# First attention: the order of four projections on the matrix engine, and of what takes them out of PSUM

## The reference

```python
# _L0_attn_ref, on hs, the 64 x 32 tokens after the conditional mix (B = 64, T = 32)
q = (hs @ Wq.T).reshape(B, T, H, DK); k = (hs @ Wk.T).reshape(B, T, H, DK)
q = _rope(q, cos, sin); k = _rope(k, cos, sin)       # x1*cos - x2*sin, x2*cos + x1*sin
v = (hs @ Wv.T).reshape(B, T, H, DV)
s = clip(hs @ Ws1.T @ Ws2.T + bs2)                    # 64 slots of each head
z = cumlogsumexp(s, axis=2); es = exp(s); enz = exp(-z)
A = where(mask, q k^T * scale, 0)
ok = enz * (A @ es); qv = softmax(ok)
W2 = where(mask, (qv * enz) @ es^T, 0); o = W2 @ v
g = (hs @ Wg.T).reshape(B, T, H, DV)
o_g = o * rsqrt(mean(o*o) + EPS) * g_norm_weight * (g * sigmoid(g))
return o_g.reshape(B, T, H * DV) @ Wo.T
```

## Time and profile before

| | us |
|---|---|
| median of 2 runs (1453.72 to 1455.73) | 1454.72 |
| the profiled execution, its own time | 1453.34 |
| span of its trace | 1451.2 |
| PE busy in it | 1329.9 (92%) |
| DVE busy | 938.1 (65%) |
| POOL busy | 556.4 (38%) |
| ACT busy | 516.8 (36%) |
| mean granted TensorE clock, as a share of full speed | 0.966 |

### The profile page before, as it was taken

The page is one execution under the profiler, slowest core; times in us unless marked ns, Lnnn a source line. Parts: engine busy times, 40 slices in busy tenths (PEclk is TensorE's granted clock), DMA queues, the critical chain, the costliest instruction groups (busy, mean ns, idle before and its releaser), DMA issues. The chain is left out here.

```text
span 1451.2 us, 36830 instructions
## 1 busy us (share of the span) xinstructions
PE 1329.9 (92%) x14806; PEld 1063.4 (73%) x14806; DVE 938.1 (65%) x1825; ACT 516.8 (36%) x1188; POOL 556.4 (38%) x608
## 2 busy tenths in 40 slices
PE   4999999999999999999985889999997789997997
PEld 3788888888888888888763667778776567775665
DVE  3787888878788778878764474252524245666786
ACT  2344444444444444444443213231322122222433
POOL 1656565565656556555532212121221111122111
PEclk9999999999999999999997899999999789997998
DMA  6000000000000000000003400000000720000620
GB/s 194 5 13 13 16 13 12 27 13 17 12 13 27 17 13 13 1 2 2 1 2 116 144 1 1 1 0 0 0 0 0 223 75 0 0 0 13 197 63 22
DMA packets 33375, 46.46 MB, mean 32 GB/s; under 512 B 6974, under 2 KB 22552, under 8 KB 32728
## 3 DMA queue, kind: packets, MB, share of 16 engines
q1 hardware_dynamic: 30888, 43.81, 9.9%
q10 hardware_dynamic: 2272, 0.52, 0.2%
q0 software_dynamic: 80, 0.26, 0.1%
HBM read 42.22 MB, written 2.36 MB: 31 GB/s over the span
## 5 line engine op out<-in xcount | busy, mean ns | idle before, releaser
L425 PE MATMUL OE<-w_o,ogT_s 128*128 128x256 f32 x512 | 137.9, 392 | 0.7 <-ACT ogT_s L513 0.7
L890 POOL TENSOR_TENSOR hT_lo<-h,hT_hi 128x512 fp32r<-128x512 f32 x44 | 56.8, 1291 | 192.6 <-ACT hT_hi L1063 192.6
L239 POOL TENSOR_TENSOR turned<-t1c,t2s 128x512 f32<-128x512 f32 x62 | 78.7, 1269 | 123.6 <-DVE t2s L650 123.6
L675 DVE RECIPROCAL enz<-SC 128x128 f32<-128x128 f32 x128 | 121.2, 947 | 0.4
L1126 DVE SCALAR_TENSOR_TENSOR t<-th,m 128x512 f32<-128x512 f32 (+1 forms) x56 | 38.4, 685 | 121.2 <-ACT th L1068 93.4
L280 POOL TENSOR_TENSOR exz<-ex,enz 128x256 f32<-128x256 f32 x64 | 47.4, 741 | 159.9 <-ACT ex L583 159.9
L324 PE MATMUL PJ<-hs_hi,w_hi 128*128 128x512 f32 x248 | 102.6, 414 | 0.0
L335 PE MATMUL PJ<-w_hi,hs_hi 128*128 128x512 f32 x256 | 101.0, 394 | 0.0
L335 PE MATMUL PJ<-w_hi,hs_lo 128*128 128x512 f32 x256 | 100.6, 393 | 0.0
L335 PE MATMUL PJ<-w_lo,hs_hi 128*128 128x512 f32 x256 | 100.5, 393 | 0.0
L324 PE MATMUL PJ<-hs_hi,w_lo 128*128 128x512 f32 x248 | 97.2, 392 | 0.0
(11 more groups left out here) (381 smaller groups left out, 3572.0 us busy)
## 6 DMA issues: line engine op xcount, KB each, us to landing
we_ring<-in_we SPq DMA_DIRECT2D x64, 256.0 KB, 3.1
w_raw<-in_w_slices SPq DMA_DIRECT2D x48, 128.0 KB, 2.1
xres<-in_x SPq DMA_DIRECT2D x2, 1024.0 KB, 8.6
turned<-in_w_slices SPq DMA_DIRECT2D x4, 512.0 KB, 4.5
out_rows<-xres SPq DMA_DIRECT2D x16, 128.0 KB, 1.7
w1r<-in_w1i SPq DMA_DIRECT2D x1, 1408.0 KB, 6.7
w_s<-in_w SPq DMA_DIRECT2D x2, 682.0 KB
w_o<-in_wo SPq DMA_DIRECT2D x1, 1024.0 KB, 5.7
```

Source lines behind the costliest of these rows:

```text
L239: pool.tensor_tensor(to[:, 0, :], x1c[:, :], x2s[:, :], ALU.subtract)
L425: m = pe.matmul(OE[:, SW:SW + D], ogT_s[:, i % 2, h * P:(h + 1) * P], w_o[:, i // G % 2, h, :], start=(h == 0), stop=(h == HQ - 1))
L675: dve.reciprocal(enz[:, cols], SC[:, SW:2 * SW][:, cols]).then_inc(z_rec, 1)
L890: eng.tensor_tensor(hT[1][s, m % 2, :], h[s, m % 2, :], hT[0][s, m % 2, :].bitcast(F32), ALU.subtract).then_inc(second, 1)
```

## The change

Three streams are written in another order. In PE's pass x1 and x2 now stand ahead of v and g, and `running` stands between v and g. The waits are set to match: before, v waited for the eviction of the x1 of the pass before, and x1 for the eviction of this pass's v; now x1 waits for the v of the pass before, and v waits for the eviction of this pass's x1 (`x1_sin` up to FIRST + i + 1). The same holds for x2 and g in PJ1. On DVE the two evictions of x2 follow those of x1 directly, the first half of `z` comes after them, and `silu` comes last. On ACT `s_high` stands ahead of `v_out`. No instruction is added or removed, and no transfer is moved.

```diff
             def x1(j):
                 if j < TURNS:
-                    pe.wait_ge(v_ev, j - FIRST + 1)
+                    pe.wait_ge(x1_sin, j)
+                    pe.wait_ge(v_ev, j - FIRST)
...
             def x2(j):
                 if j < TURNS:
-                    pe.wait_ge(g_silu, j - FIRST + 1)
+                    pe.wait_ge(x2_sin, j)
+                    pe.wait_ge(g_silu, j - FIRST)
                     quarter(j, 1, x2_mm)
 
             def proj_v(i, part):
                 if part.start == 0:
-                    pe.wait_ge(x1_sin, min(FIRST + i, TURNS))
+                    pe.wait_ge(x1_sin, min(FIRST + i + 1, TURNS))
                     pe.wait_ge(v_ev, i)
...
             def proj_g(i, part):
                 if part.start == 0:
-                    pe.wait_ge(x2_sin, min(FIRST + i, TURNS))
+                    pe.wait_ge(x2_sin, min(FIRST + i + 1, TURNS))
                     pe.wait_ge(g_silu, i)
...
                 if two:
                     slots(i + 2)
+                x1(i + 1 + FIRST)
+                x2(i + 1 + FIRST)
                 if one:
                     proj_v(i + 1, A)
-                    proj_g(i + 1, A)
-                x1(i + 1 + FIRST)
                 if two:
                     running(i + 2)
-                x2(i + 1 + FIRST)
+                if one:
+                    proj_g(i + 1, A)
...
                 if two:
                     s_e(i + 2)
+                    s_high(i + 2)
                 if one:
                     v_out(i + 1)
-                if two:
-                    s_high(i + 2)
-                if one:
                     g_t(i + 1)
...
                 if one:
                     slot_sum(i + 1)
-                    silu(i + 1)
                 if j < TURNS:
                     x1_by_cos(j)
                     x1_by_sin(j)
+                    x2_by_both(j)
                 if two:
                     z(i + 2, 0)
-                if j < TURNS:
-                    x2_by_both(j)
+                if one:
+                    silu(i + 1)
```

## The result

The changed kernel takes 1575.6 us (median of 2 runs, 1573.98 to 1577.21) against 1454.72 before: ratio 1.0838, 95% interval 1.0809 to 1.0868. The direction and the place were forecast, the size was not: 1549 was said, and 1575.6 lies outside the range of 1539 to 1562. A later set of runs of the same kernel (e6) gave 1565.53, which is also outside.

A forecast was written before the change was run, and what follows sets the result against it. The prediction took PE's own pace to bound the loop. A 1.62 us pause in 58 passes (94.0 us) plus 1.2 us for the last passes, on 1453.34, gave 1548.5, stated as 1549 us; range 1539 to 1562.

The forecast's parts named there:

- the bound and the place: The loop runs at PE's own pace; PE would pause 1.62 us a pass before v, at bank PJ0.
- what was put at nothing in the loop: Handover of x2 to g, `silu` and `pT_s` in the loop: cost 0, with covers of 0.6, 0.5 and 0.4 us.
- The last passes: Five passes without x1 and x2: `turn_p` later, 0.25 us each, 1.2 us, bounds 0 and 5 us.
- the first point of Part 1: On DVE, `t1c` starts 0.11 us after `sme` starts at 407.89, so at 408.00.
- The sum: Whole program: 1453.34 + 94.0 for 58 loop passes + 1.2 for the last passes = 1548.5 us.
- The prediction's own sign: On DVE, `t1c` starting more than 0.2 us away from 3.10 us behind `ok` would show the forecast wrong.
- Part 3: ACT's new order: `es_lo` some 0.4 us earlier, its PE wait gone, `pT_out` later; cost 0, 0.4 us cover left.
- the first pass: First loop pass, PE at half clock: twelve matmuls take about 5.5 us and cover DVE's 4.4, so no pause.
- DVE in time: Rival at bank PJ0: `t1s` ends by 407.67, PE doesn't pause, 1434 us, 1.3% less; chance 0.03.
- PE's other part shrinking: Rival, PE from `turn_p` to `slot_scores`: the pause gives others time, period grows by half as much, 1500 us; chance 0.05.
- `pT_s` late: Rival on ACT: 0.7 us later than laid out, `slot_weights` waits 0.3 us a pass, 1566 us; chance 0.04.
- the clock fall: Rival at the new handover: pauses bring PE to half clock, 1723 us, or 1583 if one pass in five; chance 0.05.

The follow-up runs named there:

- e6: Changed kernel run once more, unaltered: 1565.53 us, ratio 1.0796 to the kernel before.
- e2: Changed kernel with DVE's `sm` and `sme` moved behind the four evictions of x1 and x2: 1520.24 us, ratio 1.0480 to the kernel before.
- e3: Changed kernel with all four evictions of x1 and x2 ahead of `norm_sum`, `gated` and `slot_sum` on DVE: 1489.95 us, ratio 1.0273 to before.
- e4: Kernel before with only the ACT part of the change, `s_high` ahead of `v_out`: 1469.04 us, ratio 1.0134.
- e7: Changed kernel with a second, superfluous subtraction on POOL right ahead of `es_lo`: 1575.68 us, ratio 1.0858 to before.
- e8: Changed kernel with `sme` read from one SBUF tensor by a tensor_scalar instead of from two: 1568.25 us, ratio 1.0814 to before.
- e1: Changed kernel with POOL's `es_lo` held until DVE's `sme` is done: 1555.12 us, ratio 1.0717 to before.
- e5: Kernel before with ACT's `v_out` moved ahead of `s_e`: 1452.56 us against 1452.55, ratio 0.9998.

## Why the prediction was right and wrong

**Right: the bound and the place.** The loop ran at PE's own pace, and the new order replaced a cheap eviction of the shared bank (ACT's copy, done in time) by one that stands behind 3 us of DVE work. PE pauses once a pass in front of v. e2 and e3 give the scale: the usual period is 13.21, 12.35 and 11.81 us as 0, 0.87 and the whole of the block stand behind the evictions.

**Right: what was put at nothing in the loop.** `silu`, `pT_s` and g's handover cost nothing; in the steady passes PE has no other wait of size. The last passes cost 2.4 us together in the first profile and 0.8 in e6, for 1.2 said.

**Wrong: the start of `t1c`.** The step that failed is the first point of Part 1, "After an instruction of that size the next starts 0.11 us later", which gave `t1c` at 408.00. It was read off `mse` and `og`, and none of the rows that it used showed `sme` beside POOL's work. In the changed kernel `t1c` started 0.43 us behind `sme`, since `sme` was held by POOL's `es_lo` to its end. With the real link the sum is: 3.00 + 0.43 + 0.60 + 0.67 + 0.06 + 3.13 + 5.36 (from `turn_p` to the next `ok`) = 13.25, against 12.89. Some 0.32 of the 0.36 us is `sme`; 0.06 is PE's way from v to `turn_p`, 0.03 of it between v's first and second matmul (0.34 us, and 0.31 for x1 before), less 0.02 in small terms. Over the loop that is about 20 us. The sum gave 95.2 us for the loop and the first profile shows 114.1, which is 18.9 more; of the remaining distance to 1575.6, 5.5 us are the scatter outside the loop. The prediction's own sign says the same: `t1c` starts 3.43 us behind `ok`, where more than 0.2 us away from 3.10 was to count as wrong.

**Wrong: the range.** The parts of the prediction gave bounds of 1546 to 1564 and 6 us more for each 0.1 us in DVE's block, and the range ended at 1562: it was narrower than its own bounds. 1575.6 lies outside both.

**Wrong: what Part 3 priced.** I wrote that `s_high` ahead of `v_out` "makes `es_lo` earlier by some 0.4 us" and counted only a wait that goes. I looked at who waits for `es_lo` and never at what it would now run beside. e4 makes this shift alone and gets the long `sme`. The kernel before showed it too, where POOL and `sme` happened to meet: with `exz` in its first pass, and later with `es_lo` itself (DVE and POOL, 57 and 216 us):

```profile
57.00 0.72 POOL L280 TENSOR_TENSOR exz<-ex,enz 128x256 f32<-128x256 f32 x1
57.12 0.62 DVE L721 SCALAR_TENSOR_TENSOR sme<-sm 128x4 f32<-128x4 f32 x1
...
216.26 0.73 POOL L258 TENSOR_TENSOR es_lo<-es,es_hi 128x256 fp32r<-128x256 f32 x1 [0.35 <-ACT es_hi L525]
216.45 0.56 DVE L721 SCALAR_TENSOR_TENSOR sme<-sm 128x4 f32<-128x4 f32 x1
```

`sme` ends at 57.74 and `exz` at 57.72, then `sme` at 217.01 and `es_lo` at 216.99. Of its 64 instances in that trace 61 take 0.16 us, and three stand out: these two and one of 0.55 at 577.35, again under `es_lo`. Three outliers in a group of 64 equal instructions were the measurement that the sum needed.

The Trainium skill, SBUF — State Buffer, section "SBUF: two separate sides", states it: VectorE and GpSimd share a pair of ports as an exclusive lock, and a VectorE instruction in a 2-port mode, or one with two SBUF inputs against a GpSimd instruction that reads SBUF, is blocked while the GpSimd instruction has it. The traces agree: `sme` ends 0.01 to 0.03 us behind POOL's instruction in the changed kernel, e4, e7 and e8 (412.80 and 412.79, 402.46 and 402.43, 413.40 and 413.38, 411.52 and 411.49).

**Wrong, small: the first pass.** I let it go free, at half clock, and v paused 0.93 us there. Two things differ. The clock was back early: the stretch 58 to 60 us has 1.00, and 0.51 in the kernel before. And `sme` took 1.53 us in this pass, held over `exz` and `es_lo`; without that, x1 would have set the start of `t1c` and the pause would have been about 0.1 us (an estimate from the rows of this pass). When the clock comes back differs between executions of one kernel: e6, the same kernel, has 1.00 from 52 us on.

**The rivals.** DVE in time, PE's other part shrinking and `pT_s` late did not happen: `turn_p` to the next `ok` is 5.36 us in both kernels. Nor did the clock fall at the new handover: 58 pauses of 1.74 us with 512-column matmuls on both sides left it at 1.00. The Trainium skill, TensorE: Matmul & The Clock Gate, section "A second HAM failure mode: psum-queue depth-cycling", names short idle times between groups of matmuls as a cause of an alternating clock; these pauses show none. In the last passes, without x1 and x2, the clock did fall. The table of stretches of the changed kernel:

```profile
60.00:867.00 807.00, 697.73 (x7562) 565.54 (x7560) 573.30 (x1098) 307.13 (x791) 394.71 (x413) 1.00 0.04 10
...
869.00:871.00 2.00, 2.00 (x8) 1.52 (x6) 0.58 (x2) 0.87 (x2) 0.70 (x1) 0.51 0.00 0
```

PE waits 1.86 to 1.88 us for `es_lo` in each of the last four passes. Behind one of these waits the clock fell to half here and the pass took 12.26 us instead of 10.61; in e6 it fell behind none of the four, and in e1, with waits of 2.36 to 2.38 us, in three of four passes. That the waits bring the fall isn't shown.

## What to carry to other kernels

Where two users share a PSUM bank and only one run of matmuls lies between them, look at which engine takes the first one out and what stands in its stream ahead of that, and put the quick eviction on the tight side. When a reorder moves a GpSimd instruction, look at what VectorE does in the new place and not only at who waits for the result: a tiny SBUF-to-SBUF instruction at the end of a chain can be held for the rest of GpSimd's instruction, and sometimes for the next ones too. Held time shows as a longer busy time of the VectorE instruction and not as idle time, so no list of waits has it. An outlier in a group of otherwise equal instructions in the old trace is often the price of exactly such a meeting.

## What was not expected of the hardware

DVE's four-column instruction took 0.16 us alone and 0.46 to 0.52 us when it arrived some 0.25 us into a POOL tensor_tensor of 0.69 to 0.73 us. It was let in between two POOL instructions that follow each other in 60 passes of e7 and passed over in the first one (2.04 us). It made no difference whether it was the scalar_tensor_tensor of two SBUF tensors or the tensor_scalar of one (e8), while the reduction `sm` from SBUF kept its 0.41 to 0.42 us under POOL in every run. PE's first matmul behind a wait is followed by the second after 0.31 to 0.34 us and not 0.23, and removing the wait ahead of one run moved this loss to the next run instead of saving it (e5).
